# Moving the tokens' second scores, a key chunk and the query transposes within a hand-written order of units

## The reference

```
# layer 0, 8 heads of 40; the last 4 context rows are "tokens"
enc, ca = ctx[:, :371], ctx[:, 371:]
hs     = mha(x @ Wq, enc @ Wk, enc @ Wv)
ca_q1  = einsum('btc,th->bch', ca, Wq_ca)[:, indices]      # 112 of 192 rows
ca_hs1 = mha(ca_q1, x, x)                                  # the tokens' scores: S2
ca_hs2 = mha(ca_hs1 @ Wq, ca @ Wk_ca, ca @ Wv_ca)          # S3, p3
x1     = (hs + ca_hs2) @ Wout + b_out + x
# layer 1, 20 heads of 16
out    = mha(x1 @ Wq1, ctx @ Wk1, ctx @ Wv1) @ Wo1 + bo1 + x1
```

## Time and profile before

| | |
|---|---|
| median of 3 runs | 844.62 us (840.89 to 852.93) |
| the profiled execution | 842.08 us, its span 840.3 us |
| TensorE busy | 744.2 us (89%) |
| VectorE, ScalarE, GpSimd busy | 473.5, 396.8, 292.1 us |
| mean granted TensorE clock | 0.942 of the upper level |

### The profile page before, as it was taken

How to read it: one execution, slowest core, us unless ns; L and a number is a source line. 1 busy time by engine, 2 the same in 40 slices (tenths; PEclk the granted TensorE clock), 3 DMA queues, 4 the chain that set the end, 5 groups by cost and what they waited for, 6 DMA issues and landing times.

```text
span 840.3 us, 18167 instructions
## 1 busy us (share of the span) xinstructions
PE 744.2 (89%) x6920; PEld 637.1 (76%) x6920; DVE 473.5 (56%) x1027; ACT 396.8 (47%) x922; POOL 292.1 (35%) x401
## 2 busy tenths in 40 slices
PE   4987889898989989898998989898998989899975
PEld 4766778687778878787887878787887878788754
DVE  3632565655556656555565555565665555556652
ACT  3434445454554545455445545455454545544322
POOL 7527243342242334334232434224233433411200
PEclk9989899999999999899999999999999999999976
DMA  9327151426325161434416162422616252240400
GB/s 302 94 92 174 46 143 44 111 64 94 89 58 136 31 141 52 83 92 70 112 37 150 37 110 65 99 84 60 133 30 128 62 84 83 54 111 9 69 8 8
DMA packets 51907, 72.45 MB, mean 86 GB/s; under 512 B 11776, under 2 KB 43904, under 8 KB 51824
## 3 DMA queue, kind: packets, MB, share of 16 engines
q1 hardware_dynamic: 44784, 61.85, 30.0%
q0 software_dynamic: 6144, 9.25, 5.2%
q10 hardware_dynamic: 896, 0.20, 0.1%
HBM read 20.60 MB, written 4.26 MB: 30 GB/s over the span
## 4 chain that ended last, share of the span: by engine, by line
PE 57%; DVE 18%; ACT 15%; issue 4%; DMA 3%; ACTq 2%; SPq 0%; POOL 0%; DVEq 0%; POOLq 0%
PE bankX L972 22%; PE bankO L1192 9%; DVE negmax L758 6%; PE bankST L1160 6%; ACT arena L572 4%; PE bankS L1126 4%; ACT arena L554 3%; PE bankST L1154 3%; PE bankX L1038 2%; DVE q1T L814 2%; PE bankS L1123 2%; DVE negmax L822 2%; PE bankX L1092 2%; DVE stage L799 2%; ACT stage L602 2%
## 5 line engine op out<-in xcount | busy, mean ns | idle before, releaser
L758 DVE TENSOR_REDUCE negmax<-bankS 112x2 f32<-112x750 f32 (+1 forms) x224 | 208.7, 932 | 70.3 <-PE bankS L1126 38.5
L478 POOL DMA_DIRECT2D k_stack<-stage x192 | 96.2, 509 | 161.2 <-DVE stage L794 136.9
L1192 PE MATMUL bankO<-arena,v 125*32 125x112 f32 (+2 forms) x2688 | 120.0, 278 | 6.7 <-ACT arena L554 5.6
L554 ACT ACTIVATE arena<-bankST 125x1344 f32<-125x1344 f32 x80 | 103.5, 1293 | 33.0 <-PE bankST L1160 33.0
L1192 PEld LDWEIGHTS bankO<-arena,v 125*32 125x32 f32 (+2 forms) x2688 | 91.9, 126 | 30.8 <-issue 16.7
L1126 PE MATMUL bankS<-k_stack,q1T 112*112 112x376 f32 x320 | 91.6, 369 | 4.9 <-DVE negmax L758 4.9
L972 PE MATMUL bankX<-ctx_hi,WH 128*120 128x376 f32 (+2 forms) x192 | 75.9, 395 | 2.8 <-DVE qn L750 2.6
L572 ACT ACTIVATE arena<-bankX,negmax 112x112 f32<-112x112 f32 x128 | 43.5, 352 | 60.6 <-DVE negmax L822 60.6
L1160 PE MATMUL bankST<-q1T,k_stack 112*125 112x224 f32 x480 | 69.3, 281 | 2.3 <-DMA q1T<-mT 2.2
L972 PE MATMUL bankX<-ctx_hi,WL 128*120 128x376 f32 (+2 forms) x192 | 67.9, 353 | 0.0
L972 PE MATMUL bankX<-WH,ctx_hi 128*125 128x320 f32 x192 | 65.6, 342 | 1.1 <-ACT v L609 0.6
(11 more groups left out here) (138 smaller groups left out, 1590.0 us busy)
## 6 DMA issues: line engine op xcount, KB each, us to landing
k_stack<-stage SPq DMA_DIRECT2D x96, 176.2 KB
k_stack<-stage SPq DMA_DIRECT2D x192, 70.5 KB, 4.0
k_stack<-stage POOLq DMA_DIRECT2D x192, 47.0 KB, 3.5
ctx_raw<-in_ctxT SPq DMA_DIRECT2D x16, 376.0 KB, 3.0
k_stack<-stage SPq DMA_DIRECT2D x48, 117.5 KB
xp<-in_xpad SPq DMA_DIRECT2D x16, 224.0 KB, 3.9
x_raw<-in_xT SPq DMA_DIRECT2D x16, 168.0 KB, 2.3
out<-x1b SPq DMA_DIRECT2D x16, 140.0 KB, 3.4
```

The costliest lines, as they stand in the source:

```text
L478: pool.dma_start(dst, src).then_inc(k1_stacked_pool[b % 2], 16)
L554: nc.scalar.activation(dst[0:KC], bankST[0:KC, :, 0:GROUP * SQ], ACT.Exp).then_inc(exp_done, 1)
L758: nc.vector.tensor_reduce(negmax[:, n % 2, 2 * pair:2 * pair + 2], bankS[0:SQ, :, 0:keys], axis=AX, op=ALU.max, negate=True).then_inc(max_ ...
L1192: last = nc.tensor.matmul(dst, v, src[0:keys, c, SQ * j:SQ * j + SQ], start=(c == 0), stop=(c == NKC - 1))
```

## The change

Three things move in the table `UNITS`:

- `S2_1` goes from phase 0 of slot 3 to phase 3 of slot 2, right behind `attend`, and so ahead of K1_2;
- K1_2 goes from phase 3 of slot 2 to phase 0 of slot 3;
- `q0T_0` goes from phase 2 of slot 3 to phase 3 of slot 4, and `q0T_1` from there to phase 1 of slot 5, behind V0_0.

```diff
--- before.py
+++ after.py
@@ -46,10 +46,10 @@
 UNITS = [
     ([("V1_0", -1)], [("q1T_0", -1)], [("V1_1", -1)], [("W2", 1), ("PV2", 0)]),
     ([("q1T_1", -1), ("V1_2", -1)], [("q1T_2", -1)], [("q0", 1)], [("N1a", -2), ("K1_0", 0)]),
-    ([("K1_1", 0)], [("S3", 0)], [("N1b", -2), ("S2_0", 1)], [("K1_2", 0)]),
-    ([("S2_1", 1)], [("K0_0", 1)], [("hn1T", -2), ("q0T_0", 1)], [("K0_1", 1)]),
-    ([("K0_2", 1)], [("N0", 0), ("p3T", 0)], [("out1", -2)], [("q0T_1", 1)]),
-    ([("hn0T", 0)], [("V0_0", 1)], [("out0", 0)], [("T2_0", 1)]),
+    ([("K1_1", 0)], [("S3", 0)], [("N1b", -2), ("S2_0", 1)], [("S2_1", 1)]),
+    ([("K1_2", 0)], [("K0_0", 1)], [("hn1T", -2)], [("K0_1", 1)]),
+    ([("K0_2", 1)], [("N0", 0), ("p3T", 0)], [("out1", -2)], [("q0T_0", 1)]),
+    ([("hn0T", 0)], [("V0_0", 1), ("q0T_1", 1)], [("out0", 0)], [("T2_0", 1)]),
     ([("x1T", 0)], [("V0_1", 1), ("T2_1", 1)], [("q1", 0)], [("V0_2", 1)]),
 ]
 PHASES = range(4)
```

## The result

The changed kernel takes 812.29 us (median of 4, 803.62 to 817.05) where the kernel before takes 845.25 (median of 4): a ratio of 0.953, 95% interval 0.940 to 0.966. The ratio counts the faster executions only, for the changed kernel those of 803.62 and 808.80 us, and so is not the quotient of the medians. On a second chip it took 810.18 us, a ratio of 0.957 (0.953 to 0.962). The prediction was 793 us, 785 to 818, and faster. The sign and the range hold. The narrower forecast, 785 to 802 with a chance of 0.60, doesn't: of the 52 us between 793 and the 845.25 measured beside it, 33 came by the medians, and 38 on the second chip.

A forecast was written before the change was run, and what follows sets the result against it. TensorE bounds the kernel, with two slot 3 waits of 3.03 us per iteration and a falling clock behind them. Minus 2.4, minus 1.39, plus 0.15 give 3.64 us, times 13 is 47.3; plus 2 for iteration 1: 793 us, range 785 to 818.

The forecast's parts named there:

- Step 1: Slots 2 and 3: S2_1 before K1_2 lets eight exponentials run through; K1_2 waits some 0.9 us, shifted scores lose 0.67 us.
- Step 2: Slot 3: the waits of hn1T and q0T_0 go; attend moves from 157.61 to 154.5, minus 3.1 us.
- Step 3: Slot 4: only the row of maxima from slot 3 may come late, 0 to 1.8 us per iteration; 0.15 taken.
- the list of signs: Waits expected in the new profile; over 1 us per iteration at L1123 (slot 0) or L1160 (slot 4) refutes the forecast.
- the row of maxima lands late: Rival: the row takes 5.8 us, slot 4 waits 1.8 us per iteration, 816 us, or 834 with the clock; chance 0.13.
- two that didn't occur: Rivals within the range: clock still falls, 811 us, chance 0.10; K0's keys land late for slot 0, 807 us, chance 0.10.
- Step 4: Slot 5: q0T_1 before the second scores, and out0 waiting for V0_0's copy, cost plus 0.7 us together.
- Step 5: Key transfers start 1.33 us later; SP's chain ends at 174.4, next iteration's first scores at 174.7: hidden by 0.3 us.
- The clock: With slot 3's waits gone the granted clock stays at 0.99 to 1.00, gaining 1.39 us per iteration.

The follow-up runs named there:

- the late transfers, the run in which the rows met no crowd: Changed kernel with GpSimd's 12 key transfers moved behind its split of x: 794.01 us, ratio 0.937 to the kernel before.
- its two halves: Changed kernel with query transposes left in slots 3 and 4: 816.49 us; kernel before with only the query transposes moved: 827.13 us.
- the last order: Changed kernel with GpSimd's transfers behind the split of x, plus K1_2 behind the shifted scores, hn1T behind attend, three SP transfers given to GpSimd: 791.10 us.

## Why the prediction was right, and where it was not

- **Step 1, the eight exponentials and the wait of K1_2: right.** They run from 248.20 on without a break, and the copy of K1_2 follows at 250.87, 2.67 us later; I had 2.66. The wait is 0.80 us, 14 times; I had about 0.9. The run with the transposes alone shows the other side: with K1_2 ahead of `S2_1` the chain of the earlier trace rows starts late as before, and `hn1T` waits 1.33 us.
- **Step 2, slot 3: right to a tenth.** From K1_2 to `attend` I had 3.96 us (150.54 to 154.5) and it takes 3.90 (249.70 to 253.60). The split of K1_2 starts SP's transfers 2.29 us behind K1_2's start; I had 2.26.
- **Step 3, slot 4: the place was wrong, and the size.** The row that I feared for, sent in slot 3 and used in slot 4, has 4.0 us and is never late. The one sent in slot 4 and used in slot 5 is. I took for granted that a row which is in time now stays so where the distance to its user stays the same, and looked only at the one whose distance shrank. Its distance is still 3.6 us, but it now leaves 6.9 us behind the start of K1's stackings where it left 11.5 us behind (162.94 against 151.49 in the frame of the prediction, by the timeline of ScalarE), since slot 3 takes 3 us less and the stackings begin later. So it meets the crowd of both queues, and takes up to 5.6 us. The sum had 0.15 us per iteration. The rows' waits are 15.8 us in iterations 2 to 13 of the first profile, 1.3 per iteration, and 12.2 us in those of the second, 1.0 (waits of 0.3 us and more). This is the term that was mis-sized. By the list of signs a wait of over 1 us per iteration at L1160 meant that the forecast was wrong, though it named slot 4. The rival "the row of maxima lands late" had the mechanism, a price of up to 1.8 us per iteration and 816 us, with a chance of 0.13; only its slot is another. That the range held is owed in part to the room it left for this rival and for two that didn't occur.
- **The Trainium skill's** fixed cost of about 2.0 us ("DMA: Bandwidth & Descriptors", Anatomy of one DMA) would have left this term at 0, and the prediction 2 us further off. That section gives it for GpSimd's path, and the row goes by ScalarE's queue, so it was not a price for this transfer. Here the same row was in time after 3.6 us in one iteration and took 5.6 us in another, and the waits went when GpSimd's transfers were moved: a constant can't describe it.
- **Step 4, slot 5: right.** From `hn0T` to `attend` of slot 5 it takes 4.32 us (262.31 to 266.63) instead of 3.55 (166.32 to 169.87 before): plus 0.77, where I had 0.7.
- **Step 5, SP's chain: right.** "Hidden, but by a hair": L1123 waits once in iteration 1 of the first profile, for 1.17 us, and in iterations 1 and 2 of the second, for 0.64 and 0.49. It is no bound from iteration 3 on. That `issue` is what the profile names there doesn't rule out a transfer.
- **The clock: largely right.** In iterations 2 to 13 the stretches below 0.99 are 10 of 12 before, 2 in the first profile after, 1 in the second, and none with the late transfers. The iterations of 49 us are those in which a row waited longest. Behind K1_2's 0.8 us it fell in none of the profiles.
- **The start: not foreseen.** The first K1 stacking began 6.1 us later in the first profile after (71.86 against 65.79), with the same program up to there: the clock stood at 0.53 from 20 to 40 us instead of 0.91. I had laid the spread of the runs to how often the clock falls in the iterations. Between the two profiles of the changed kernel, 815.79 and 809.01 us, 6.0 of the 6.8 us lie ahead of the first K1 stacking. How much of that is the clock was not separated: with the clock at 1.00 in that stretch, one run's first stacking still began at 69.71.

The sum for iterations 2 to 13: 12 times 3.64 is 43.7 us forecast; 24.3 and 27.5 us measured in the two profiles; 43.1 us (575.91 less 532.80) in the run in which the rows met no crowd. Of the 19.4 us missing in the first profile 15.8 are waits for rows, and most of the rest is the clock in iterations 3 and 12: each is 4.9 to 5.0 us longer than the undisturbed one, and 3.2 to 3.3 of that are waits.

## What to carry to other kernels

A stall upstream also spaces out the transfers: before taking it away, list every small transfer downstream with the distance to its user, and ask what will be in flight when it leaves, not only whether its own distance shrinks. Bulk transfers that are not urgent belong in the stretch where nothing small is waited for; here that was worth 16 us, and nothing before the change. And an order table can be costed by walking one undisturbed iteration: the change and its two halves came out within 0.1 us per undisturbed iteration. It gives the order's own waits, and not what transfers do to each other: that is where the change and the last order missed.

## What the runs showed of the hardware

- A transfer of one row (1.8 KB) between two places in on-chip memory, issued on ScalarE's queue, was used without a wait 3.60 us after its issue in one iteration and took 5.61 us in another. GpSimd's twelve key transfers had all been issued 0.4 us before the first row left, and were still being issued when the second did.
- Two things go with the length of the first wait, in the two profiles of the changed kernel. In the iterations in which GpSimd paused between its sixth and seventh transfer (3, 6, 9 and 12) it was 1.3 to 2.0 us. In the others it followed the pace of SP's twelve: no wait where they took 9.1 us or more, 0.2 to 1.0 us where they took 8.1 to 8.7, and 1.1 to 1.4 us where they took 7.8 to 7.9. The pace alone does nothing: with GpSimd's transfers behind the split of `x`, SP's twelve took under 7.8 us in iterations 3, 7, 10 and 12, and no row was late in slot 5. What sets the pace, and what makes GpSimd pause, stays open.
- SP's transfers for K1 (70.5 KB each) took 3.8 to 4.1 us from issue to landing at the median in the seven profiles in which GpSimd's twelve were issued beside them, and 2.6 us in the four in which these came later.
- The clock fell to its lower level (0.50) behind waits of 1.34 and 1.69 us that stood close together, in 10 of 12 iterations of the kernel before, and behind waits of 1.34 and 0.73 us in 7 of 12 with the query transposes alone. Behind a single row's wait it fell after 1.78 and 2.01 us in the first profile of the changed kernel and after 1.79 and 1.59 us in the second, and stayed up after 1.67 us in the first. With the transfers beside layer 0's keys it fell after 1.44 us in iteration 1 and stayed up after 2.04 us in iteration 14. So the length of the wait doesn't settle it by itself. It never fell behind K1_2's 0.8 us.
- The start has the same instructions in all these kernels but the one with a third of layer 0's keys, and yet the first K1 stacking began anywhere from 65 to 77 us in the twelve profiles. In the six in which it began after 71 us the granted clock was 0.50 to 0.57 from 20 to 40 us; in the others it was 0.83 to 1.00.
